# Cross-attention scores: the exponential's bias computed on ScalarE instead of VectorE, and the probabilities kept as 16-bit patterns, moved in pairs

## The reference

```python
def _fq_sym(x, axis):
    s = max(max(abs(x), axis) / 127.0, 1e-08)
    return clip(round(x / s), -127.0, 127.0) * s

def _fq_unsigned(x, axis):
    s = max(max(x, axis) / 255.0, 1e-08)
    return clip(round(x / s), 0.0, 255.0) * s

q = ((x @ Wq + bq) * scale).reshape(1, B * N, H, hd)   # 1024 tokens, 16 heads of 32
k, v = (cond @ Wkv + bkv)                              # 2048 keys for every token
q, k, v = _fq_sym(q, -1), _fq_sym(k, -1), _fq_sym(v, 2)
attn = softmax(einsum('bhqd,bhkd->bhqk', q, k))
attn = _fq_unsigned(attn, -1)                          # whole numbers 0 to 255, times a step
out = einsum('bhqk,bhkd->bhqd', attn, v) @ Wp + bp
```

## Time and profile before

| what | value |
|---|---|
| median of the runs | 1244.13 us (1243.3 to 1245.73, 3 runs) |
| the profiled execution | 1247.11 us |
| its span | 1245.4 us |
| TensorE busy | 1007.9 us, 81% of the span |
| VectorE busy | 849.3 us, 68% |
| ScalarE busy | 704.1 us, 57% |
| GpSimd busy | 244.6 us, 20% |
| mean granted TensorE clock | 0.948 |

### The profile page before, as it was taken

One profiled execution on the slowest core, in us unless ns is written; L12 is line 12 of the kernel. 1 busy time (PEld: TensorE's weight loads), 2 busy tenths in 40 slices (PEclk: granted clock), 3 DMA queues, 4 the chain that ended last, 5 costly groups with the idle time before them and its releaser, 6 DMA issues. The chain is left out here.

```text
span 1245.4 us, 21873 instructions
## 1 busy us (share of the span) xinstructions
PE 1007.9 (81%) x8049; PEld 684.2 (55%) x8049; DVE 849.3 (68%) x1401; ACT 704.1 (57%) x1046; POOL 244.6 (20%) x216
## 2 busy tenths in 40 slices
PE   4988987899547677777777777777679989999998
PEld 3744734788436444444444444444557765566566
DVE  6756735999688799999999999999661531111126
ACT  2354352355516799999999999999323202121221
POOL 1134043565360200000000000000533620000014
PEclk9998999899769699999999999999779989999999
DMA  8200002310000100000000000000030395232215
GB/s 322 92 1 1 1 1 82 106 51 17 9 1 1 43 2 2 2 0 0 0 0 0 0 0 0 0 0 0 1 149 27 112 377 241 68 111 68 68 55 182
DMA packets 24854, 68.14 MB, mean 55 GB/s; under 512 B 2722, under 2 KB 6818, under 8 KB 23778
## 3 DMA queue, kind: packets, MB, share of 16 engines
q1 hardware_dynamic: 20114, 52.48, 11.2%
q0 software_dynamic: 4400, 14.42, 3.6%
q10 hardware_dynamic: 288, 0.52, 0.2%
HBM read 49.07 MB, written 18.35 MB: 54 GB/s over the span
## 5 line engine op out<-in xcount | busy, mean ns | idle before, releaser
L1315 DVE TENSOR_REDUCE cs_top<-cs_s_b 128x1 f32<-128x512 f32 x256 | 164.7, 685 | 16.5 <-PE cs_s_b L1344 7.6
L1352 PE MATMUL cs_tp<-ident,cs_p_int 128*128 128x128 f16 x2048 | 159.3, 221 | 8.4 <-ACT cs_pT L1295 3.3
L1303 DVE TENSOR_REDUCE cs_top<-cs_s_a 128x1 f32<-128x1024 f32 x128 | 155.5, 1215 | 7.7 <-PE cs_s_a L1344 7.6
L1289 ACT ACTIVATE cs_p_int<-cs_s_b,cs_bias,cs_step_now 128x1024 int16<-128x1024 f32 x128 | 154.1, 1204 | 11.2 <-DVE cs_bias L1322 5.0
L1352 PEld LDWEIGHTS cs_tp<-ident,cs_p_int 128*128 128x128 f16 x2048 | 122.8, 98 | 61.2 <-issue 46.8
L1344 PE MATMUL cs_s_b<-k_parts,q_int 96*128 96x512 bf16 x256 | 79.1, 391 | 92.2 <-ACT cs_p_int L1289 91.8
L1289 ACT ACTIVATE cs_p_int<-cs_s_a,cs_bias,cs_step_now 128x1024 int16<-128x1024 f32 x128 | 152.8, 1194 | 0.0
L1295 ACT CAST cs_pT<-cs_tp 128x1024 bf16<-128x1024 int16 x128 | 129.5, 1012 | 4.4 <-PE cs_tp L1352 3.7
L2161 PE MATMUL ff_h<-ff_experts,ff_zgT 128*128 x368 | 115.0, 466 | 0.9 <-ACT ff_zgT L1800 0.9
L1448 POOL TENSOR_TENSOR co_o<-co_o,v_step 128x512 f32<-128x512 f32 x8 | 10.7, 1334 | 467.8 <-DVE co_o L1470 467.8
L1344 PE MATMUL cs_s_a<-k_parts,q_int 96*128 96x512 bf16 x256 | 79.9, 395 | 22.4 <-ACT cs_p_int L1289 18.1
(11 more groups left out here) (277 smaller groups left out, 2105.9 us busy)
## 6 DMA issues: line engine op xcount, KB each, us to landing
ff_experts<-in_experts_dram SPq DMA_DIRECT2D x8, 2176.0 KB, 15.1
slots<-sa_zero SPq DMA_DIRECT2D x1, 5888.0 KB, 24.6
ff_zg<-slots POOLq DMA_DIRECT2D x23, 256.0 KB, 2.9
run_y<-ff_yv SPq DMA_DIRECT2D x23, 256.0 KB, 2.0
ff_raw<-in_weights_dram SPq DMA_DIRECT2D x6, 768.0 KB, 6.0
ck_raw<-in_ctxT_dram SPq DMA_DIRECT2D x8, 512.0 KB, 3.4
stage<-in_cwkv_dram SPq DMA_DIRECT2D x2, 1024.0 KB, 6.8
out_dram<-x_res SPq DMA_DIRECT2D x8, 256.0 KB, 2.0
```

What stands on the lines that cost most here:

```text
L1289: nc.scalar.activation(p_int[:, u, half * HALF:(half + 1) * HALF], s[:, :], ACT.Exp, bias=bias[:, u:u + 1], scale=step_now[:, h:h + 1], ac ...
L1303: nc.vector.tensor_reduce(top[:, u, 0:1], s_a[u][:, :], AX_X, ALU.max).then_inc(max_ok, 1)
L1315: nc.vector.tensor_reduce(top[:, u, 1 + c:2 + c], s_b[:, c * 512:(c + 1) * 512], AX_X, ALU.max).then_inc(max_ok, 1)
L1352: ins = nc.tensor.transpose(tp[:, k, :], p_int[:, u, key:key + P].bitcast(F16), ident16[:, :])
```

## The change

Three things change in `cross_scores`.

1. The bias moves. VectorE's `tensor_scalar` goes, and so does its copy of the negative steps. ScalarE now computes the bias as an activation with the function Identity on the 128x1 maximum, with the negative step as scale and a column of ln 255 (`cs_ln_pmax`, filled once by GpSimd) as bias. It waits for `top_ok` and stands directly in front of the upper exponential, which waits for it through `bias_ok`. ScalarE copies the negative steps too, once for each tile.
2. The probabilities keep their 16-bit patterns. `cs_pT` becomes int16, and TensorE reads it as half-precision floats: the whole number p is then the float p * 2^-24. `v_int` becomes half precision as well, and the product is multiplied by 2^24 when it leaves PSUM.
3. ScalarE's copy of the upper half reads and writes 32-bit integers, two probabilities at once: 512 elements for each partition in place of 1024. VectorE's copy of the lower half keeps its 1024 elements, now int16 to int16.

```diff
-        pT = sb("cs_pT", [P, 2, KT, P], BF16)
+        pT = sb("cs_pT", [P, 2, KT, P], I16)
+        ln_pmax = sb("cs_ln_pmax", [P, 1], F32)
...
         @block.gpsimd
         def _(pool):
+            nc.gpsimd.memset(ln_pmax[:, :], LN_PMAX).then_inc(ln_ok, 1)
...
                     nc.scalar.copy(step_now[:, :], q_step[:, t, :]).then_inc(act_tile, 1)
-                    act.wait_ge(act_tile, 2 * t + 1)
+                    nc.scalar.copy(nstep_now[:, :], q_nstep[:, t, :]).then_inc(act_tile, 1)
+                    act.wait_ge(act_tile, 3 * t + 2)
                 for half, s, made, used in ((1, s_b, eb_ok, tb_ok), (0, s_a[u], ea_ok, ta_ok)):
                     if half:
+                        act.wait_ge(top_ok, n + 1)
+                        nc.scalar.activation(bias[:, u:u + 1], top1[:, u:u + 1], ACT.Identity, bias=ln_pmax[:, 0:1],
+                                             scale=nstep_now[:, h:h + 1]).then_inc(bias_ok, 1)
                         act.wait_ge(bias_ok, n + 1)
...
-                nc.scalar.copy(pT[:, u, HKT:KT, :], tp[:, :, :].bitcast(I16)).then_inc(rb_ok, 1)
+                nc.scalar.copy(pT[:, u, HKT:KT, :].rearrange("p k q -> p (k q)").bitcast(I32),
+                               tp[:, :, :].rearrange("p k q -> p (k q)").bitcast(I32)).then_inc(rb_ok, 1)
...
-                    if h == 0:
-                        if at_least(n, H):
-                            v_.wait_ge(bias_ok, n)
-                        nc.vector.tensor_copy(nstep_now[:, :], q_nstep[:, t, :]).then_inc(dve_tile, 1)
-                        v_.wait_ge(dve_tile, t + 1)
...
                     v_.wait_ge(max_ok, 3 * n + 3)
+                    if at_least(n, 2):
+                        v_.wait_ge(bias_ok, n - 1)
                     nc.vector.tensor_reduce(top1[:, u:u + 1], top[:, u, :], AX_X, ALU.max).then_inc(top_ok, 1)
-                    v_.wait_ge(top_ok, n + 1)
-                    if at_least(n, 2):
-                        v_.wait_ge(ea_ok, n - 1)
-                    nc.vector.tensor_scalar(bias[:, u:u + 1], top1[:, u:u + 1], nstep_now[:, h:h + 1], LN_PMAX,
-                                            ALU.mult, ALU.add).then_inc(bias_ok, 1)
...
-                    nc.vector.tensor_copy(o_raw[:, t - 1, :], out[:, :]).then_inc(out_read, 1)
+                    nc.vector.tensor_scalar(o_raw[:, t - 1, :], out[:, :], P_UNIT, None, ALU.mult).then_inc(out_read, 1)
...
-                        ins = nc.tensor.matmul(out[:, head * D:(head + 1) * D], pT[:, u, k, :],
+                        ins = nc.tensor.matmul(out[:, head * D:(head + 1) * D], pT[:, u, k, :].bitcast(F16),
...
-        v_int = sb("v_int", [P, KT, C], BF16)
+        v_int = sb("v_int", [P, KT, C], F16)
```

More of the change, by code:

```diff
@@ L35 @@
 LN_PMAX = log(PMAX)
+P_UNIT = 2.0 ** 24
 Q_FLOOR = 1e-08
@@ L1226, in cross_scores @@
         max_ok = sem("max_ok")
+        ln_ok = sem("ln_ok")
         top_ok = sem("top_ok")
         act_tile = sem("act_tile")
-        dve_tile = sem("dve_tile")
         w_in = sem("w_in")
@@ L1272, in keep_sums @@
                 nc.scalar.copy(z_sum[:, t, :, :], z_now[:, :, :]).then_inc(act_tile, 1)
-                act.wait_ge(act_tile, 2 * t + 2)
+                act.wait_ge(act_tile, 3 * t + 3)
             def step(t, h, n):
@@ L1294, in step @@
                     act.wait_ge(av_ok, n - 1)
-                nc.scalar.copy(pT[:, u, HKT:KT, :], tp[:, :, :].bitcast(I16)).then_inc(rb_ok, 1)
+                nc.scalar.copy(pT[:, u, HKT:KT, :].rearrange("p k q -> p (k q)").bitcast(I32),
+                               tp[:, :, :].rearrange("p k q -> p (k q)").bitcast(I32)).then_inc(rb_ok, 1)
+            act.wait_ge(ln_ok, 1)
             units(act, step)
```

## The result

| | before | after |
|---|---|---|
| median of the runs, side by side | 1244.93 us (4 runs) | 1264.98 us (4 runs) |
| ratio | | 1.0165, 95% interval 1.0138 to 1.0191 |
| the profiled execution, its span | 1247.11, 1245.4 us | 1262.85, 1261.1 us |
| first to last upper exponential (the score loop) | 413.88 to 874.77: 460.9 us | 409.27 to 890.44: 481.2 us |
| median distance of two upper exponentials | 3.54 us | 3.71 us |

The forecast was 1274 us, with a range of 1262 to 1286. The loop is 20 us longer. In the profiled pair the span grew by less, 15.7 us, because the loop begins 4.6 us earlier after parts that the change doesn't touch, self-attention among them; between 100 and 150 us TensorE was granted 0.94 of its clock in the one execution and 1.00 in the other. Behind the last upper exponential they need 370.6 and 370.7 us.

A forecast was written before the change was run, and what follows sets the result against it. The prediction took a ring of waits through cs_s_b, not a busy engine, as the bound. Bias on ScalarE +33.3 us, second heads -2.9, tile starts -0.3: +30 on the 1244.1 median, so 1274 us, range 1262 to 1286.

The forecast's parts named there:

- the ring: Score loop's chain of waits through cs_s_b, from one upper exponential to the next: claimed to set the whole 3.54 us period.

The follow-up runs named there:

- bits_only: Kernel before plus only the 16-bit patterns, paired copy and scaled output, bias still on VectorE: 1240.65 us against 1244.68, ratio 0.9972; repeated, 0.9968.

## What to carry to other kernels

Before work is moved from a busy engine to a less busy one, follow one period from the buffer that closes it and add up start-to-start distances. If the sum is the period, moved work is worth only its length as a link, pointer operands and hand-overs included, and the link can be longer on the engine that seems free. Look for a second ring as well, over two periods where a buffer is double. Work shortened beside the ring pays only where the ring does not bind or where another move uses the room: 0.42 us a head on ScalarE gave 0.3% alone, most of it at the tiles' starts, and 0.7% with the output's copy moved into it. And a hand-over should be read in an ordinary iteration, not at the loop's edge, where other instructions carry the wait.

## What the runs showed of the hardware

- A wait that hangs on ScalarE's compute instruction costs 0.03 us from the end of the operation waited for, also when that is ScalarE's own; with a register or an empty instruction carrying it, 0.09 to 0.11.
- A 128x1 operation on ScalarE takes 0.191 (copy), 0.203 (constants), 0.294 (one pointer), 0.387 us (two).
- ScalarE moves 1024 16-bit patterns of at most 255 as 512 32-bit integers from PSUM in 0.586 us, against 1.012 one by one. A copy of 512 floats took 0.585, so in these three rows the time goes by elements, not by bytes. VectorE's copy takes 0.68 us with bfloat16 or int16 as its output.
- Half-precision matmuls of these patterns take the 177 ns of the bfloat16 ones (L1379 after, L1378 before).
- TensorE's granted clock over the same stretch of the loop was 0.98 and 1.00 at a period of 3.54 us (the kernel before, bits_only), 0.97 at 3.71 and 0.83 at 3.94.
